# A two-block transformer layer on one core: first attention pairs loaded from the parts on chip, spills issued by ScalarE, bias load moved, sparse preparation reordered with the local keys on GpSimd

## The chip, the cores and the metric

The kernel runs on one core of a Trainium2 chip. The metric is the device time of one execution in microseconds. The kernel before takes 1689.7 us, the median of 3 runs (1689.04 to 1690.89).

## What is computed

An input x of 2 x 1024 tokens with 128 features goes through three blocks, each added to x:

```python
x = x + 0.5 * ffn(layernorm(x))     # dense attention (16 heads of 8) + mixture of experts
x = x + attn(layernorm(x))          # sparse attention: index scores, top 96 keys per query, 8 heads
x = x + 0.5 * ffn(layernorm(x))
```

`ffn` computes `h = layernorm(x + attention(x) @ w_o)`, routes each token to the best 2 of 8 experts (128 to 512 to 128, gelu) and normalizes again. `attn` scores keys with 4 small heads (relu of q.k, weighted sum), takes 64 local keys and the 32 best others, and attends over these with a compressed key and a rotated part: softplus of a projection, turned by an angle that depends on the position. All data are fp32.

## The kernel before, in words

The program runs a dense block (`c` = 0), the sparse block, and the dense block again (`c` = 1). Each engine has its own instruction list in a fixed order, written out by hand; semaphores tie them together. SP's queue issues nearly all DMAs, in the order of `sp_ffn` and `sp_sel`, and a wait of SP holds back every DMA behind it.

**Dense block.** The tokens are normalized and turned, then projected. `act_ffn` copies each projection's high part to `qparts`/`kparts` (L1244) and VectorE computes the low part (L1621, `low_done`); the values are copied by ScalarE (L1250, `va_ready`). Attention runs over 16 pairs of heads (8 per batch, `PAIRS`) with a ring of 4 buffers `QB`, `KB`, `VS`. In the buffers each head has 32 rows, the products of two parts of q with two parts of k, and 3 rows for the maxima. The rows are got by way of memory: `sp_spill` (L492) writes all parts of one batch to `q_rows` and `k_rows` (L496, L497), and `sp_rows` (L466) reads a pair back, repeated (L475, L476), with three zero rows (L477) and the values (L482). SP spills batch 0, waits for it, loads pairs 0 and 1, spills batch 1, and loads pairs 2 and 3. GpSimd (`pool_fill`) clears the buffers first (`filled`).

Per pair TensorE computes the scores once for the maxima (`pe_pass1`, L772, L779; 9 units), VectorE reduces them (`dve_max`, L1468, L1478; L1486 gives the row maxima), GpSimd splits the maxima into three bf16 parts, TensorE turns them, ScalarE copies them (`act_maxrow`, L1218), and `sp_maxrows` (L485) loads them with two small DMAs (L489) into the ring buffer. Then TensorE computes the shifted scores (`pe_scores`, L805), ScalarE the exponentials (L1209), GpSimd cuts the diagonals (L711), and TensorE multiplies with the values (`pe_values`, L827). Before the loop, pass 1 runs for 9 units of pair 0 and 4 of pair 1. In the loop, pass 1 of pair `it + 2` runs beside the scores of pair `it`.

After attention come the projection, a normalization, the gate and the experts. ScalarE waits for the experts' biases (`bb1_loaded`), which `sp_sel_loads` loads in the first block (L566, L567, five DMAs of single elements), before it turns the second normalization. The first two experts' weights are loaded at the kernel's start, for `c` = 1 as soon as the sparse block is done.

**Sparse block, preparation.** Queries are made in four rounds (`pe_raw_queries`, `act_round`, `act_log`, `dve_magnitudes` L1808, `pe_swap` L1105, `dve_rotated` L1817 to L1823, `sp_round` L600): the softplus is split into |x|, a log of exp (`act_log`, two table loads and two passes) and a maximum; `sp_round` places the four heads' parts into `QALL` with 16 DMAs of 128 KB. `pe_index`, `act_index` (L1400) and `dve_select` (L1840, L1871 to L1875) score and select keys; their units with negative places run in the preparation. The keys by row (`KVS`) go to memory for the gathers. The keys by column (`KTB`, `KTR`, a part of `QALL`) are turned by `dve_local_keys` (L1788) on VectorE after the selection of the second tile and before rounds 2 and 3; it waits for `kt_log`. GpSimd waits for the stored keys and the first indices, and then issues the gathers (L750). The main loop (`pe_keys`, `pe_scored`, ...) starts when all queries are placed.

The lines that set this order in the preparation of VectorE:

```python
for u in early[1][1:]:
    dve_select(dve, u)
dve_local_keys(dve)
for n in range(B, 2 * B):
    dve_magnitudes(dve, n)
    dve_rotated(dve, n)
```

## Time and profile before

| | |
|---|---|
| median of 3 runs | 1689.7 us |
| the profiled execution's own time | 1688.96 us |
| its span, first to last instruction | 1686.8 us |
| TensorE (matmul) / VectorE / ScalarE / GpSimd busy | 83% / 74% / 58% / 27% of the span |
| first dense block, attention | 0 to 303 us |
| sparse block | 535 to 1156 us, main loop from 685 |
| second dense block, attention | 1157 to 1450 us |
| chain that ended last | PE 55%, DVE 13%, ACT 10%, DMA 6%, issue 6%, SPq 5% |

PE is TensorE's matmul and PEld its weight load, DVE VectorE, ACT ScalarE, POOL GpSimd, SP the engine that issues DMAs; an engine's name with q is its instruction queue, whose DMA issues are not busy time. The chain is the profile's own: from the last instruction back to what released each step. A releaser is inferred. L12 is line 12 of the kernel. Times in the trace are microseconds from the span's start.

### The profile page before, as it was taken

The numbers are of one execution on the slowest core, as the hardware profiler recorded it, in microseconds if no ns is written. First come the engines' busy times: TensorE is split into PE (matmuls) and PEld (weight loads), VectorE is DVE, ScalarE is ACT, GpSimd is POOL, SyncE is SP. The second block draws the span as 40 slices with busy tenths as digits, with TensorE's granted clock in tenths as the row PEclk, the third lists the DMA queues.
The fourth block names the chain that finished last, engine by engine and source line by source line (L and its number), as shares of the span: only waits on it lengthen the run. The fifth ranks groups of instructions, "written<-read, shape, count | busy, mean of one in ns | idle before, by whom it ended". The sixth has DMA issues, their size and how long they took to land.

```text
span 1686.8 us, 31737 instructions
## 1 busy us (share of the span) xinstructions
PE 1401.3 (83%) x10664; PEld 915.3 (54%) x10664; DVE 1243.8 (74%) x2568; ACT 976.6 (58%) x1788; POOL 447.8 (27%) x751
## 2 busy tenths in 40 slices
PE   3599999799994754789999989996399999799994
PEld 2355554577773311456656655675255555577773
DVE  4578886698778577677878887754478887488787
ACT  2166666478883672346455555552166666488883
POOL 4122222100002023245455445622222233100000
PEclk9599999799997965899899999997599999799998
DMA  5211110022202244122122122212311110022200
GB/s 143 95 48 45 43 47 11 1 102 76 75 26 78 47 121 112 30 61 61 36 80 73 38 61 63 74 36 81 110 33 47 46 47 18 2 102 75 75 25 25
DMA packets 65020, 99.72 MB, mean 59 GB/s; under 512 B 21109, under 2 KB 44853, under 8 KB 62840
## 3 DMA queue, kind: packets, MB, share of 16 engines
q1 hardware_dynamic: 55254, 80.43, 15.5%
q0 software_dynamic: 8192, 16.79, 3.9%
q8 instruction: 75, 1.23, 0.3%
q10 hardware_dynamic: 1440, 0.80, 0.2%
q14 instruction: 59, 0.47, 0.1%
HBM read 73.39 MB, written 10.69 MB: 50 GB/s over the span
## 4 chain that ended last, share of the span: by engine, by line
PE 55%; DVE 13%; ACT 10%; DMA 6%; issue 6%; SPq 5%; DVEq 4%; ACTq 1%; POOL 0%; POOLq 0%
PE twin L973 8%; PE twin L963 5%; PE twin L827 5%; PE twin L1142 5%; PE twin L805 5%; DMA ffn<-arena 4%; PE twin L772 4%; ACT arena L1209 4%; DVEq L1830 2%; ACT experts L1279 2%; PE twin L1170 2%; PE twin L1158 2%; PE twin L1123 2%; PE twin L1186 2%; ACT arena L1277 2%
## 5 line engine op out<-in xcount | busy, mean ns | idle before, releaser
L1209 ACT ACTIVATE arena<-twin 128x1024 f32<-128x1024 f32 x288 | 293.8, 1024 | 172.7 <-PE twin L805 170.8
L750 POOL DMA_INDIRECT arena<-kv_rows,IDX x256 | 251.6, 983 | 309.9 <-PE twin L1189 151.0
L1478 DVE TENSOR_REDUCE arena<-twin 128x8 f32<-128x1024 f32 (+1 forms) x160 | 195.3, 1225 | 77.2 <-PE twin L772 42.9
L1277 ACT ACTIVATE arena<-twin,bias 128x512 f32<-128x512 f32 x256 | 184.9, 722 | 60.6 <-PE twin L963 60.6
L1527 DVE TENSOR_TENSOR experts<-arena,experts 128x512 fp32r<-128x512 f32 x256 | 170.1, 689 | 61.8 <-ACT experts L1279 60.5
L963 PE MATMUL twin<-experts,experts 128*128 128x512 f32 x768 | 197.0, 403 | 6.1 <-ACT experts L1279 6.1
L772 PE MATMUL twin<-ffn,ffn 64*128 64x128 f32 (+3 forms) x1152 | 154.8, 351 | 50.5 <-DMA arena<-arena 27.7
L1468 DVE TENSOR_REDUCE arena<-twin 128x2 f32<-128x1024 f32 x128 | 152.9, 1222 | 51.8 <-PE twin L772 48.4
L1279 ACT ACTIVATE experts<-twin,bias 128x512 fp32r<-128x512 f32 x256 | 186.2, 727 | 0.0
L973 PE MATMUL twin<-experts,experts 128*128 128x512 f32 x768 | 183.3, 390 | 1.0 <-DVE experts L1527 1.0
L711 POOL TENSOR_SCALAR_AFFINE_SELECT arena<-arena 128x256 f32<-128x256 f32 x256 | 99.6, 407 | 307.6 <-ACT arena L1209 307.6
L805 PE MATMUL twin<-ffn,ffn 64*128 64x128 f32 (+3 forms) x960 | 148.4, 373 | 27.7 <-DMA ffn<-arena 22.7
L963 PEld LDWEIGHTS twin<-experts,experts 128*128 128x128 f32 x768 | 143.2, 192 | 51.1 <-ACT experts L1279 23.7
L973 PEld LDWEIGHTS twin<-experts,experts 128*128 128x128 f32 x768 | 143.9, 188 | 32.9 <-issue 2.6
L827 PE MATMUL twin<-arena 128*32 128x128 f32 (+3 forms) x1920 | 159.2, 432 | 2.6 <-POOL arena L711 1.6
L645 POOL TENSOR_TENSOR rstd<-vareps,neghalf 128x8 f32<-128x8 f32 x14 | 23.4, 1674 | 511.7 <-DVE vareps L1457 511.7
L772 PEld LDWEIGHTS twin<-ffn,ffn 64*128 64x128 f32 x1152 | 96.7, 201 | 83.9 <-ACT arena L1209 36.1
L805 PEld LDWEIGHTS twin<-ffn,ffn 64*128 64x128 f32 x960 | 79.2, 188 | 109.0 <-issue 62.4
L1894 DVE TENSOR_TENSOR HN<-twin,RT 96x512 f32<-96x512 f32 x128 | 86.9, 680 | 59.1 <-PE twin L1142 51.4
L1429 ACT ACTIVATE ATT<-twin,col 128x256 f32<-128x256 f32 x128 | 60.6, 473 | 104.9 <-DVE col L1903 104.0
L1435 ACT ACTIVATE ATT<-ATT,inverse 128x256 f32<-128x256 f32 x128 | 64.6, 505 | 81.3 <-DVE inverse L1908 80.8
L1142 PE MATMUL twin<-XN,arena 128*128 128x512 bf16 x408 | 104.2, 395 | 0.2 <-DVE HN L1894 0.2
(258 smaller groups left out, 2186.6 us busy)
## 6 DMA issues: line engine op xcount, KB each, us to landing
arena<-wt_rows SPq DMA_DIRECT2D x16, 1024.0 KB, 4.8
arena<-in_L_ffn_w SPq DMA_DIRECT2D x32, 256.0 KB, 5.2
ffn<-q_rows SPq DMA_DIRECT2D x64, 128.0 KB
ffn<-k_rows SPq DMA_DIRECT2D x64, 128.0 KB
XT<-idx_rows SPq DMA_DIRECT2D x16, 512.0 KB, 4.1
q_rows<-ffn SPq DMA_DIRECT2D x8, 512.0 KB, 4.9
k_rows<-ffn SPq DMA_DIRECT2D x4, 1024.0 KB, 9.2
arena<-HN SPq DMA_DIRECT2D x32, 128.0 KB, 2.4
```

The source lines that it names most:

```text
L750: pool.indirect_dma_start(G[d % GR][:, g, :], None, kv_rows, bass.IndirectOffsetOnAxis(ap=IDX[:, q, k * GB + g:k * GB + g + 1], axis=0))\
L772: m = pe.matmul(bank[2 * slot + s][:, at * P:(at + blocks) * P], QB[buf][r, q * P:(q + 1) * P], KB[buf][r, k0 * P:(k0 + blocks) * P], star ...
L805: x = pe.matmul(bank[2 * slot + s][:, at * P:(at + 4 - p) * P], KB[buf][r, kc * P:(kc + 1) * P], QB[buf][r, (4 * g + p) * P:(4 * g + 4) * ...
L827: m = pe.matmul(bank[6][r:r + STRIP, p * P:], VS[buf][:, v:v + STRIP], PT[(UNITS * buf + u) % PT_RING][:, s, at * P:(at + 4 - p) * P], sta ...
L963: m = pe.matmul(bank[f][:, :], W1R[buf][w][:, f * P:(f + 1) * P], XR[x][:, tb * BANK:(tb + 1) * BANK], start=((w, x) == pairs[0]), stop=(( ...
L973: m = pe.matmul(bank[4 + k][:, :], W2R[buf][w][:, f, :], H1R[k][x][:, f, :], start=(f == 0 and (w, x) == pairs[0]), stop=(f == FC - 1 and ...
L1142: m = pe.matmul(o[:, :], TAB[part][:, 4 * b + c, :], OH[OH_AT[x][c] % OHR][:, :], start=(c == 0 and part == 0), stop=(c == n - 1 and part ...
L1209: act.activation(PT[(UNITS * buf + u) % PT_RING].rearrange("p s n -> p (s n)"), twin[2 * u % S_RING][:, :], ACT.Exp, scale=float(HD) ** -0 ...
L1277: act.activation(H1[tb % 2][:, f, :], bank[f][:, :], ACT.Gelu_apprx_tanh, bias=bias1[buf][:, f:f + 1])
L1279: act.activation(H1R[tb % 2][0][:, f, :], bank[f][:, :], ACT.Gelu_apprx_tanh, bias=bias1[buf][:, f:f + 1]).then_inc(gelu_done, 1)
L1478: dve.tensor_reduce(to, scores.rearrange("p (s t k) -> p s t k", s=2, t=to.shape[2]), AX_X, ALU.max).then_inc(max_done, 1)
L1527: dve.tensor_tensor(H1R[tb % 2][1][:, f, :], H1[tb % 2][:, f, :], H1R[tb % 2][0][:, f, :].bitcast(F32), ALU.subtract)\
```

## The change

It does six things.

1. The first four pairs of each dense block are no longer read back from memory. `sp_first` copies them from `qparts` and `kparts` on chip to `QB` and `KB`, eight DMAs of 16 rows (64 KB) per pair, each as soon as the low parts that it needs are ready. For pairs 0 and 1 the rows have semaphores of their own (`first_loaded`), and the values follow when both pairs' rows are issued; TensorE waits for the values in front of the first `pe_values`. The order on SP is: pairs 0, 1, their values, pair 2 with values, the maxrows of pair 0, pair 3 with values. The zero rows aren't loaded for these pairs.
2. The spill of both batches is issued by ScalarE (`act_spill`), behind its value copies and ahead of `act_maxrow(0)`. SP waits for it in front of the loop over the other pairs.
3. The bias load moves from the start to the end of the first block's attention in SP's order (`sp_biases`). In block 2 the loads of the first two experts' weights move behind pair 3.
4. For `c` = 1, buffer 0 is filled by ScalarE (`act_fill`) and not by GpSimd, and GpSimd drains before it waits for the sparse block's end.
5. In the sparse preparation the swap of round 0, the log of round 0, round 1 of the queries and its log, and the log of the keys change places with index and select units.
6. The local keys move from VectorE (16 instructions of 512 columns) to GpSimd (`pool_local_keys`, 8 instructions of 1024 columns), in front of the gathers; SP's rounds 2 and 3 wait for them.

```diff
+FIRST_LOADS = 16 * 2 * 2 * PARTS
+VISITS = PAIRS // RING
+
+def rows_target(c, buf, visit):
+
+    first = 16 if buf < 2 else 16 + FIRST_LOADS
+    return (ROW_LOADS * (VISITS - 1) + first) * c + first + ROW_LOADS * visit
...
+        def sp_parts(sp, it, s, which, done):
+            h, n = slice((2 * it + s) * HD, (2 * it + s + 1) * HD), HD * PARTS
+            for i in range(PARTS):
+                r = TILE * s + i * n
+                if which == 0:
+                    to, rows = QB[it], qparts[h, i, 0:L].unsqueeze(1).broadcast_to([HD, PARTS, L])
+                else:
+                    to, rows = KB[it], kparts[h, :, 0:L]
+                sp.dma_start(to[r:r + n, :].bitcast(F32), rows.bitcast(F32)).then_inc(done, 16)
+        def sp_values(sp, it, buf):
+            va = VA[:, :, :, :, :].rearrange("p a s k d -> p (a s k d)")
+            n = 2 * TB * VW
+            sp.dma_start(VS[buf][:, 0:n], va[:, bass.ds(it * n, n)]).then_inc(rows_loaded[buf], 16)
+        def sp_first(sp, c, it, done):
+            if c and it == 0:
+                sp.wait_ge(first_filled, 1)
+            else:
+                sp.wait_ge(filled, RING * c + it + 1)
+            for which in range(2):
+                sp.wait_ge(low_done, 8 * c + 2 * (which + 1))
+                for s in range(2):
+                    sp_parts(sp, it, s, which, done)
...
-        def sp_spill(sp, c, b):
...
         def sp_ffn(sp, c):
-            if c:
-
-                sp.wait_ge(x_ready, 2)
-                sp_expert(sp, c, 0, 0)
-                sp_expert(sp, c, 1, 1)
-
             if c == 0:
                 sp.wait_ge(zeroed, 1)
                 sp.dma_start(zero_rows, PT[0][0:MAXROWS, :, :].rearrange("p s n -> p (s n)")).then_inc(zero_stored, 16)
-            sp_spill(sp, c, 0)
+            for it in range(2):
+                sp_first(sp, c, it, first_loaded[it])
+            sp.wait_ge(va_ready, NG * (c + 1))
+            for it in range(2):
+                sp_values(sp, it, it)
             sp.wait_ge(zero_stored, 16)
-            sp.wait_ge(rows_spilled[0], (PARTS + 1) * 16 * (c + 1))
-            for k in range(RING):
-                if k == 2:
-                    sp_spill(sp, c, 1)
-                sp.wait_ge(filled, RING * c + k + 1)
-                sp_rows(sp, c, k, k)
-            sp.wait_ge(rows_spilled[1], (PARTS + 1) * 16 * (c + 1))
+            sp_first(sp, c, 2, rows_loaded[2])
+            sp_values(sp, 2, 2)
             sp_maxrows(sp, c, 0, 0)
+            sp_first(sp, c, 3, rows_loaded[3])
+            sp_values(sp, 3, 3)
+            if c:
+                for e in range(2):
+                    sp_expert(sp, c, e, e)
+            for b in range(B):
+                sp.wait_ge(rows_spilled[b], (PARTS + 1) * 16 * (c + 1))
             with sp.Fori(1, PAIRS // RING) as i:
                 for k in range(RING):
                     sp_maxrows(sp, c, i * RING + k - (RING - 1), (k + 1) % RING)
                     sp_rows(sp, c, i * RING + k, k)
             for it in range(PAIRS - RING + 1, PAIRS):
                 sp_maxrows(sp, c, it, it % RING)
+            if c == 0:
+                sp_biases(sp)
...
         def sp_round(sp, n):
...
             if n >= B:
 
+                sp.wait_ge(kl_ready, 1)
                 sp.wait_ge(qr_ready, 2 * (n + 1))
...
             if c:
-
+                pool.drain()
                 pool.wait_ge(x_ready, 2)
...
-                pool.memset(QB[buf][:, :].bitcast(F32), 0.0)
-                pool.memset(KB[buf][:, :].bitcast(F32), 0.0)
...
+                if c == 0 or buf:
+                    pool.memset(QB[buf][:, :].bitcast(F32), 0.0)
+                    pool.memset(KB[buf][:, :].bitcast(F32), 0.0)
...
+            pool_local_keys(pool)
...
+        def pool_local_keys(pool):
+            lo, mid = P // 2, P // 2 + DR
+            pool.wait_ge(kt_log, 1)
+            pool.wait_ge(rot_ready, 1)
+            for b in range(B):
+                pool.tensor_tensor(KTB[:, b, :], KTB[:, b, :], KTR[:, b, :], ALU.add)
+            pool.drain()
+            for b in range(B):
+                up, down, far = QALL[lo:mid, NH // 2 + 2 + b, 0:L], QALL[mid:, NH // 2 + 2 + b, 0:L], QALL[lo:mid, NH // 2 + b, 0:L]
+                pool.tensor_tensor(up, up, ROT[lo:mid, 0, :], ALU.mult)
+                pool.tensor_tensor(far, down, ROT[mid:, 1, :], ALU.mult)
+            pool.drain()
+            for b in range(B):
+                up, far = QALL[lo:mid, NH // 2 + 2 + b, 0:L], QALL[lo:mid, NH // 2 + b, 0:L]
+                m = pool.tensor_tensor(KL[ROWKV:, b, LW:], up, far, ALU.add)
+            m.then_inc(kl_ready, 1)
+            pool.drain()
...
-                pe.wait_ge(rows_loaded[buf], ROW_LOADS * (PAIRS // RING * c + visit + 1))
+                if isinstance(it, int) and it < 2:
+                    pe.wait_ge(first_loaded[it], FIRST_LOADS * (c + 1))
+                else:
+                    pe.wait_ge(rows_loaded[buf], rows_target(c, buf, visit))
...
                 pe_next(pe, c, 1, 1, u, u + EARLY, 0)
+            for it in range(2):
+                pe.wait_ge(rows_loaded[it], rows_target(c, it, 0))
...
+            pe_swap(pe, 0)
             for u in early[0:NIH]:
                 pe_index(pe, u)
-            pe_swap(pe, 0)
             for q in range(4):
                 if q < 2:
                     pe.wait_ge(qt_ready, q + 1)
...
                     m = pe.matmul(bank[2 + q % 2][:, t * P:t * P + ROWKV], XT[:, (4 * q + t) * P:(4 * q + t + 1) * P], WKV[:, :],
                                   start=True, stop=True)
                 m.then_inc(kv_done, 1)
+            pe.wait_ge(kv_c, 4)
+            pe_raw_queries(pe, 1)
             for u in early[NIH:]:
                 pe_index(pe, u)
-            pe.wait_ge(kv_c, 4)
-            pe_raw_queries(pe, 1)
...
+        def act_fill(act):
+            act.wait_ge(x_ready, 2)
+            for rows in (QB[0], KB[0]):
+                act.activation(rows[:, :], spare[:, 0:1].broadcast_to([P, L]), ACT.Copy)
+            act.drain()
+            for s in range(2):
+                r = slice(TILE * s + PRODS, TILE * s + ROWS)
+                m = act.activation(KB[0][r, :], neghalf[r, 0:1].broadcast_to([ROWS - PRODS, L]), ACT.Copy, scale=-2.0)
+            m.then_inc(first_filled, 1)
+        def act_spill(act, c):
+            for b in range(B):
+                act.wait_ge(low_done, 8 * c + 8 // B * (b + 1))
+                pairs, t = slice(b * (PAIRS // B), (b + 1) * (PAIRS // B)), slice(b * L, (b + 1) * L)
+                for r in range(PARTS):
+                    act.dma_start(q_rows[pairs, :, r].rearrange("j s d t -> (j s) d t"), qparts[:, r, t].bitcast(F32)).then_inc(rows_spilled[b], 16)
+                act.dma_start(k_rows[pairs].rearrange("j s d r t -> (j s d) r t"), kparts[:, :, t].bitcast(F32)).then_inc(rows_spilled[b], 16)
         def act_ffn(act, c):
             n_turn = (0, 4)[c]
+            if c:
+                act_fill(act)
...
                 m.then_inc(va_ready, 1)
+            act_spill(act, c)
             act_maxrow(act, c, 0)
...
-                if n == 3:
+                if n == 1:
                     act_log(act, (MU[0],)).then_inc(mu_log, 1)
             act.wait_ge(sg_ready, 1)
             act.wait_ge(padded, 1)
...
                 act.activation(KVS[:, rows, 0:2 * DR], src[:, :, 0:2 * DR], ACT.Abs)
                 act.activation(KVS[:, rows, 2 * DR:ROWKV], src[:, :, 2 * DR:ROWKV], ACT.Copy)
                 act.activation(KVR[:, rows, :], src[:, :, 0:2 * DR], ACT.Relu).then_inc(kv_c, 1)
+            act_round(act, 1)
+            for u in early[NIH:2 * NIH]:
+                act_index(act, u)
             act_log(act, (KVS[:, :, 0:2 * DR],)).then_inc(kv_log, 1)
-            for u in early[NIH:]:
+            act_log(act, (MU[1],)).then_inc(mu_log, 1)
+            for u in early[2 * NIH:]:
                 act_index(act, u)
-            act_round(act, 1)
-            act_log(act, (MU[1],)).then_inc(mu_log, 1)
...
+            for u in early[0][2:8]:
+                dve_select(dve, u)
             dve.wait_ge(kv_log, 1)
             dve.tensor_tensor(KVS[:, :, 0:2 * DR], KVS[:, :, 0:2 * DR], KVR, ALU.add).then_inc(kv_ready, 1)
-            for u in early[0][2:]:
+            for u in early[0][8:]:
                 dve_select(dve, u)
             dve_magnitudes(dve, 1)
             dve_select(dve, early[1][0])
             dve_rotated(dve, 1)
             for u in early[1][1:]:
                 dve_select(dve, u)
-            dve_local_keys(dve)
```

## Rows read from the trace of the kernel before

**Rows 1.** Waits, engine PE: engine line waited for, total us, times, longest us.
```profile
PE twin L772 <- DMA arena<-arena: 27.7, 2, 14.2
...
PE twin L805 <- DMA ffn<-arena: 22.7, 7, 10.8
```

**Rows 2.** Timeline, 0 to 110 us: start us, us, engine, line, operation, [idle before it].
```profile
22.54 2.62 SPq L566 DMA_DIRECT2D biases<-in_L_ffn_bb  x4
...
24.76 0.69 DVE L1621 TENSOR_TENSOR ffn<-twin,ffn 128x512 fp32r<-128x512 f32 x1 [0.17 <-ACT ffn L1244]
...
28.46 3.48 ACT L1250 ACTIVATE arena<-twin 128x128 f32<-128x128 f32 x16 [0.29 <-PE twin L889]
...
45.33 1.65 PE L772 MATMUL twin<-ffn,ffn 64*128 64x512 f32 x6 [14.23 <-DMA arena<-arena]
```

**Rows 3.** Chain that ended last: start us, us, what; DMA pieces run to their landing.
```profile
27.71 7.07 DMA k_rows<-ffn
38.64 6.56 DMA arena<-arena
...
60.68 9.11 DMA ffn<-arena
...
99.08 2.21 DMA ffn<-arena
...
673.74 4.99 DMA arena<-XN
```

**Rows 4.** Timeline, 58 to 102 us.
```profile
59.42 0.27 ACT L1218 ACTIVATE arena<-twin 48x128 f32<-48x128 bf16 x1 [27.48 <-PE twin L788]
...
69.84 0.80 PE L805 MATMUL twin<-ffn,ffn 64*128 64x512 f32 x2 [10.46 <-DMA ffn<-arena]
```

**Rows 5.** Windows: length; PE, PEld, DVE, ACT, POOL busy; clock, DMA share, GB/s.
```profile
32.00:34.00 2.00, 0.00 (x0) 0.00 (x0) 0.00 (x0) 0.00 (x0) 1.84 (x4) 1.00 0.87 354
...
62.00:64.00 2.00, 0.00 (x0) 0.00 (x0) 0.00 (x0) 0.00 (x0) 0.00 (x0) 0.50 0.15 56
...
72.00:74.00 2.00, 1.74 (x12) 1.12 (x12) 1.74 (x3) 1.33 (x2) 0.42 (x1) 0.50 0.00 0
```

**Rows 6.** Timeline of the second block's start, 1144 to 1225 us.
```profile
1175.76 3.48 ACT L1250 ACTIVATE arena<-twin 128x128 f32<-128x128 f32 x16 [0.29 <-PE twin L889]
...
1191.83 1.65 PE L772 MATMUL twin<-ffn,ffn 64*128 64x512 f32 x6 [13.43 <-DMA arena<-arena]
...
1205.86 0.27 ACT L1218 ACTIVATE arena<-twin 48x128 f32<-48x128 bf16 x1 [26.62 <-PE twin L788]
...
1216.59 0.80 PE L805 MATMUL twin<-ffn,ffn 64*128 64x512 f32 x2 [10.76 <-DMA ffn<-arena]
```

**Rows 7.** Timeline of the sparse preparation, 600 to 705 us.
```profile
615.72 1.91 ACT L1292 ACTIVATE arena<-arena 64x2048 f32<-64x2048 f32 x1
...
624.30 1.06 ACT L1292 ACTIVATE ATT<-ATT 128x1024 f32<-128x1024 f32 x1
...
625.68 0.69 DVE L1794 TENSOR_TENSOR arena<-arena 64x512 f32<-64x512 f32 x1
...
637.62 1.29 DVE L1808 SCALAR_TENSOR_TENSOR ATT<-twin,ATT 128x512 f32<-128x512 f32 x2
...
652.86 1.29 DVE L1808 SCALAR_TENSOR_TENSOR ATT<-twin,ATT 128x512 f32<-128x512 f32 x2
...
671.84 2.50 SPq L600 DMA_DIRECT2D arena<-XN  x4
...
684.98 1.94 PE L1136 MATMUL twin<-const,arena 128*128 128x128 f32 x8 [18.80 <-DVE arena L1728]
```

**Rows 8.** Page, part 6, DMA issues: count, KB each, us to landing.
```profile
arena<-HN SPq DMA_DIRECT2D x32, 128.0 KB, 2.4
```

**Rows 9.** Timeline, 520 to 612 us, engine POOL.
```profile
547.62 1.52 POOL L735 CAST maskb<-arena 128x1280 bf16<-128x1280 f32 x1
```

**Rows 10.** Page, part 5, costliest groups: count, busy us, mean ns, idle before.
```profile
L711 POOL TENSOR_SCALAR_AFFINE_SELECT arena<-arena 128x256 f32<-128x256 f32 x256 | 99.6, 407 | 307.6 <-ACT arena L1209 307.6
```

49 lines of the change are left out of this document (14 added, 35 removed).

## The prediction, made before the change was run

> **What bounds the kernel now.** I first read the list of waits, engine PE: two of its largest sums are transfers, 27.7 us in two waits of L772 and 22.7 us in seven of L805 [rows 1]. The long ones occur once per dense block, at its start, so I read the timeline there, then the chain of waits to see whether they lie on it.
>
> First block. ScalarE copies the last projection (V) until 28.46+3.48 = 31.94 (the last va_ready), and TensorE starts pass 1 only at 45.33 [rows 2]. Between them lie: SP busy with the bias DMAs from 22.54, the spill, its landing (7.07 us from the k_rows issue at 27.71) at 34.8, the row loads of pairs 0 and 1, and the landing of the values issued at 38.64 [rows 2, 3]. All these are in the chain. Then nine and four units of pass 1 (pairs 0 and 1) are paced by VectorE's maxima. ScalarE copies the turned maxima at 59.42, but L805 runs only at 69.84: the two small maxrow DMAs take 9.11 us from the second issue, while later pairs take 2.21 [rows 3, 4]. While they wait, the mean busy share of the 16 DMA engines is 0.15, against 0.87 while the spill lands [rows 5]. 0.15 of 16 is 2.4 engines: a backlog on very few engines, not a full bus. The second block repeats it: V copied by 1175.76+3.48 = 1179.24, pass 1 at 1191.83, maxima out at 1205.86+0.27 = 1206.13, L805 at 1216.59 [rows 6].
>
> Sparse preparation. The chain runs through VectorE from 625.68 (dve_local_keys) to 637.62, where dve_magnitudes(2) starts, though ScalarE had its input ready at 624.30+1.06 = 625.36. From there rounds 2 and 3 follow: 652.86 magnitudes(3), then SP's placing DMAs one after another, landed 4.99 us after the issue at 673.74, and the main loop at 684.98 [rows 3, 7].
>
> **Direct loads of the first pairs.** Removed from the path: spill, its landing, and the reload. Added: eight SBUF-to-SBUF DMAs of 64 KB per pair on SP. Nearest row: placing copies of 128 KB on SP cost 2.50/4 = 0.6 us of issue each and land in 2.4 us [rows 7, 8]. First block: the biases leave SP's queue at 22.54, the zero row store takes 0.5, so SP is ready at 23.0. Q parts wait for the second low half, two units before the fourth, about 23.7, then 4 x 0.6 = 2.4 to 26.2; the K parts' low halves are done at 24.76+0.69 = 25.45 [rows 2], so K follows to 28.6 and lands at 28.6+2.4 = 31.0. That is before 31.94, so the V copy becomes what comes last: pass 1 at 32.2 instead of 45.33, that is 13.1 saved. Second block: the same counting puts the last K copy at about 1178.5, before 1179.24; pass 1 at 1179.5 instead of 1191.83, 12.3 saved. The bounds: if the copies land as slowly as the values did (6.56 [rows 3]) the start is 35.2 and 3 us per block are lost; the V copy excludes more gain than counted.
>
> Pair 1 is wanted nine maxima later (45.33 to about 55 before, so near 42 now). Its eight issues end at 33.6 and land near 36 to 38. The values of pairs 0 and 1 now follow at 35; they are needed only at the first pe_values, so moving them costs nothing. Pair 2 is issued by 40, pair 3 after the maxrow DMAs, by 53, needed near 75. The expert weights of block two, moved behind these, are needed 200 us later. Nothing waits for them.
>
> Here the question is how many engines one such copy uses, since that decides the backlog. The rows show the k_rows reload as the thing queued on about two engines [rows 5]. The Trainium skill, DMA: Bandwidth & Descriptors, section Why a DMA increments its semaphore by 16 and not by 1, says that a copy runs on the largest number up to 16 that divides both patterns' slowest dimension. By that rule the k_rows reload (slowest dimension 2) runs on two engines, with which the trace agrees, and the new copies (8 source rows) on eight; the sum would stay as it stands.
>
> **The maxrow wait.** The copy of the maxima is now at 59.42+0.27-13.1 = 46.6. In front of the maxrow DMAs on SP there is nothing pending (pair 2 landed near 43; no k_rows reload). The spill (4 MB) is now on ScalarE's queue from 31.94. At the 354 GB/s that the spill reached [rows 5], 4 MB and the 1.1 MB of pairs 1 and 2 with values take 5.1/0.354 = 14.4 us: gone at about 47 to 48. A normal maxrow load takes two issues and 2.21, together about 3.1 from the copy [rows 3]. So L805 at about 50 instead of 69.84: 7.0 more. Second block: 1206.13+3.1 = 1209.3 against 1216.59, 7.3 more. Bounds: it still waits as long as before (0 gained), or all 7 come back. I take all, since the few-engine backlog is absent. Per block 13.1+7.0 = 20.1 and 12.3+7.3 = 19.6, together 39.7.
>
> **Spill issued by ScalarE.** Behind it on ScalarE is act_maxrow(0), wanted at 46.3. Six issues of 0.6 to 1.5 us are about 5.6 us, 31.94 to 37.5; a full queue can stretch this to perhaps 43. Then it costs nothing; if the cover is gone, a few us. The first reader of the spilled rows is pair 4, after pair 0's values.
>
> **Fill of buffer 0 on ScalarE, early drain on GpSimd.** Four copies of 1024 columns, about 1 us each, while VectorE normalizes the input (7 us) and ScalarE would only wait; hidden. GpSimd fills buffer 1 before SP, busy with pair 0 until about 1176, gets to it. Cost 0 to 1.
>
> **Bias load** at the end of the first block's attention: five issues (3.2 us) on an SP that next waits for the expert weights' table; ScalarE needs it some 15 us later. Cost 0.
>
> **Sparse preparation.** Removed from VectorE: 637.62-625.68 = 11.9 us on the path [rows 7]. Reordered: the swap of round 0 before the index units, the log of round 0 two copies earlier, round 1 before the second index group. I followed these: rotated(0) gains 3.5, but the KVS log delays the second index group, ScalarE must still do two logs before the last four index units, and the K turn starts only about 1 us sooner. So local keys' input (kt_log, before 615.72+1.91 = 617.6) comes at 616.7, and magnitudes(2) starts at about 624.6 instead of 637.62: 13.0. The bounds of the reordering alone are 0 and 3.5; I take 1.1.
>
> Added on GpSimd: eight two-input instructions of 1024 columns, for which the trace has no row. Bounds from the nearest: the cast, 1.52 for 1280 columns, gives 1.2 each, 10 us [rows 9]; the affine selection, 407 ns for 256 columns, gives 1.6 each, 13 us [rows 10]; twice the latter, since there are two inputs, 26 us. I take 13, the fp32 row: kl_ready near 630 (627 to 643). It gates SP's round 2, which needs rotated(2) anyway, done just before magnitudes(3), now at 652.86-13 = 639.9. So it is hidden except at the upper end, where 3 are lost. The gather behind it on GpSimd starts there; the main loop wants its first two loads at 672, 40 us later. The Trainium skill, GPSIMD Engine Reference, section Performance versus the Vector engine, gives 4.5 us for such an instruction of 2048 columns: estimated 18 us in all, kl_ready at 635, still hidden.
>
> Net 12: 13 less 1 for instructions of VectorE and GpSimd that may hold each other up.
>
> **Sum.** 39.7 + 12 = 51.7 on the profiled execution's 1688.96 (span 1686.8 and 2.2 around it): 1637.3. The median of the runs is 0.7 above it: 1638.
>
> **Rivals.**
> 1. The sparse gain is mostly lost: GpSimd's adds and multiplies and VectorE's two-input ones slow each other, so that kl_ready or magnitudes(3) comes late. Four two-input operations of VectorE in round 2, each held up by 1.2 us, and kl_ready at 643 (3 us) give 8 lost: 1646. Against: the rest of round 2 reads PSUM. Chance 0.17. The Trainium skill, SBUF — State Buffer, section SBUF: two separate sides, states such an exclusive lock between the two engines; no row here shows it.
> 2. The maxrow load still waits, now behind the spill, or ScalarE stands in its own full queue: 5 to 7 lost per block, 1648 to 1652. For: 4 MB are in flight at 46. Against: the bus carries 354 GB/s. Chance 0.13.
> 3. More than counted: the granted clock stays at its upper level after the short waits. The stretch after 69.84 ran at 0.50 [rows 5], its matmuls up to twice as long; I estimate 2 us per block, and with a reordering worth 3.5 that gives 1631. Chance 0.12.
> 4. Slower: a direct copy is served by one engine. One engine of the late backlog carried 56/2.4 = 23 GB/s [rows 5], so 64 KB take 2.8 us, a pair 22. Pair 0 lands at 48, pair 1 at 70 (wanted at 57), and the maxrow load stands behind pair 2 until 92 instead of 69.84: 22 later per block, less 12: 1690+44-12 = 1722. With three pairs in front of the maxrow load it turns slower above 1.8 us a copy. Against: [rows 8], the same kind of copy at 2.4 us. Chance 0.03.
> 5. The change does not do what it says, for instance pass 1 waits for something I missed at 45; 12 remains, or nothing: 1678 to 1690. Chance 0.02.
>
> The forecast, 1632 to 1644, has 0.53. The range reaches from 1628 to 1652. It takes in most of rivals 1 to 3 and leaves out 4 and 5. A measurement of this kernel can tell about 0.2% (3.4 us) from no change; faster 0.96, same 0.01, slower 0.03.
>
> **What would show it.** Pass 1 at about 32 and, in the second block, 12 us sooner after the V copy; the wait of L805 for its transfer at 3 to 4 us each; the k_rows issues on ScalarE's queue; eight GpSimd TENSOR_TENSOR of 1.2 to 3.3 us; magnitudes(2) right behind the selection's last step; the main loop near 652 on the new clock of time (684.98-20-13). Wrong would be: a wait of L772 for its rows above 3 us, a wait of SP's round 2 on GpSimd, or ScalarE's maxrow copy late.

## The result, and the profile after

The changed kernel takes 1669.99 us (median of 4 runs, 1667.76 to 1671.85), the kernel before 1690.05 us beside it (4 runs): a ratio of 0.9881, 95% interval 0.9864 to 0.9898. The gain is 20 us where 52 were forecast, and the time lies outside the range of 1628 to 1652.

The page of after, its first parts:

```profile
span 1666.0 us, 31709 instructions
...
PE 1392.9 (84%) x10630; PEld 911.5 (55%) x10664; DVE 1235.5 (74%) x2552; ACT 980.9 (59%) x1792; POOL 463.5 (28%) x755
...
PE 54%; DVE 12%; ACT 10%; issue 6%; SPq 6%; DMA 4%; DVEq 4%; POOL 1%; ACTq 1%; POOLq 0%
```

The waits of TensorE in after, from 20 to 75 us (us in total, times, longest), which answer to [rows 1]:

```profile
PE twin L827 <- DMA ffn<-ffn: 11.9, 2, 8.6
PE twin L860 <- DMA ffn<-arena: 5.2, 1, 5.2
```

L827 is pass 1 (L772 before), L860 the scores (L805 before). The longest wait of pass 1 fell from 14.2 to 3.31 us, but a second one of 8.6 us is new. The timeline of TensorE and ScalarE in after, first block (start, us, instruction, idle before), which answers to [rows 2, 3]:

```profile
34.32 1.06 PE L827 MATMUL twin<-ffn,ffn 64*128 64x512 f32 x6 [3.31 <-DMA ffn<-ffn]
...
52.96 1.65 PE L827 MATMUL twin<-ffn,ffn 64*128 64x512 f32 x6 [8.60 <-DMA ffn<-ffn]
...
55.80 0.29 PE L843 MATMUL twin<-ident_b,arena 128*128 128x128 bf16 x1
56.12 0.27 ACT L1275 ACTIVATE arena<-twin 48x128 f32<-48x128 bf16 x1 [24.28 <-PE twin L843]
61.29 0.80 PE L860 MATMUL twin<-ffn,ffn 64*128 64x512 f32 x2 [5.21 <-DMA ffn<-arena]
```

Pass 1 starts at 34.32 instead of 45.33, and then stands at pair 1 until 52.96. The transpose of pair 0's maxima (L843) comes behind pair 1's four units in TensorE's order, so it is held back too: the maxima are copied at 56.12, not at 46.6 as forecast, and the first scores start at 61.29, not at 50. Why pair 1 is late stands in the two DMA queues of after, SP's and ScalarE's:

```profile
23.72 22.21 SPq L484 DMA_DIRECT2D ffn<-ffn  x16
45.97 4.68 SPq L489 DMA_DIRECT2D arena<-arena  x2
50.77 6.73 SPq L484 DMA_DIRECT2D ffn<-ffn  x8
...
58.17 1.64 SPq L520 DMA_DIRECT2D ffn<-arena  x2
...
31.05 0.66 ACTq L1311 DMA_DIRECT2D q_rows<-ffn  x1
...
32.40 3.38 ACTq L1312 DMA_DIRECT2D k_rows<-ffn  x1
35.82 3.58 ACTq L1311 DMA_DIRECT2D q_rows<-ffn  x2
39.42 2.89 ACTq L1312 DMA_DIRECT2D k_rows<-ffn  x1
```

The 16 direct copies of pairs 0 and 1 (L484) take 22.21 us of SP's time. The eight of pair 0 are issued in 6.7 (0.67 to 1.14 each). The eight of pair 1, from 30.55 on, take 15.4, while the spill is issued and in flight: two still take 0.67 and 0.71, one 1.09, and five 1.84 to 3.04. SP then still has values and pair 2 in front of the maxrow load (L520), which it issues at 58.17, 1.8 us behind the copy of the maxima (56.39).

The second block repeats it: pass 1 at 1167.82, a wait of 8.91 us for pair 1 until 1186.76, first scores at 1195.58. Before, the first scores came 37.3 us behind the last V copy [rows 6], now 30.2 us behind it (1165.35): 7.1 gained of 19.6 forecast.

The account against before, from the starts of the same instructions in both traces (the last line is the span itself):

| | before | after | change, total | forecast, total |
|---|---|---|---|---|
| pass 1, block 1 | 45.3 | 34.3 | -11.0 | -13.1 |
| first scores, block 1 | 69.8 | 61.3 | -8.6 | -20.1 |
| last scores, block 1 | 298.3 | 293.3 | -5.0 | -20.1 |
| first compressed-query matmul | 548.5 | 541.3 | -7.2 | -20.1 |
| main loop of the sparse part | 685.0 | 670.3 | -14.7 | -32 |
| first scores, block 2 | 1216.6 | 1195.6 | -21.0 | -51.7 |
| span | 1686.8 | 1666.0 | -20.8 | -51.7 |

So the dense blocks gave about 7 us each (20.1 and 19.6 forecast), the sparse preparation 7 (12 forecast). Single landmarks carry a noise of 1 to 3 us. In four more traces with the same instructions up to there (three of them of kernels with an edited sparse part) pair 1 is late as well and the first scores of block 1 start at 61.6 to 64.5. The stretch from first to last scores takes 228.3 to 232.3 us in them; it takes 228.4 before and 232.0 here, so the 3.6 us that seem to be lost on the way are within that noise.

### The profile page after: what moved, and what is told of

It reads as the page before. It is cut to its first block, busy times and chain, and to the rows that moved or that the text cites. A ratio compares the mean times of both kernels' runs of the same rounds, so it can differ in the third digit from the quotient of the medians.

```text
span 1666.0 us, 31709 instructions
## 1 busy us (share of the span) xinstructions
PE 1392.9 (84%) x10630; PEld 911.5 (55%) x10664; DVE 1235.5 (74%) x2552; ACT 980.9 (59%) x1792; POOL 463.5 (28%) x755
## 3 DMA queue, kind: packets, MB, share of 16 engines
q8 instruction: 75, 1.23, 0.3%
## 4 chain that ended last, share of the span: by engine, by line
PE 54%; DVE 12%; ACT 10%; issue 6%; SPq 6%; DMA 4%; DVEq 4%; POOL 1%; ACTq 1%; POOLq 0%
PE twin L1030 9%; PE twin L1020 5%; PE twin L882 5%; PE twin L1199 5%; PE twin L860 5%; PE twin L827 4%; DMA ffn<-arena 4%; ACT arena L1266 3%; SPq L484 3%; DVEq L1897 3%; ACT experts L1359 2%; PE twin L1227 2%; PE twin L1215 2%; PE twin L1180 2%; ACT arena L1357 2%
## 5 line engine op out<-in xcount | busy, mean ns | idle before, releaser
L1266 ACT ACTIVATE arena<-twin 128x1024 f32<-128x1024 f32 x288 | 294.1, 1024 | 165.9 <-PE twin L860 164.1
L1560 DVE TENSOR_REDUCE arena<-twin 128x8 f32<-128x1024 f32 (+1 forms) x160 | 195.4, 1225 | 67.6 <-PE twin L827 33.2
L827 PE MATMUL twin<-ffn,ffn 64*128 64x128 f32 (+3 forms) x1152 | 154.7, 351 | 44.5 <-DMA ffn<-ffn 24.1
L860 PE MATMUL twin<-ffn,ffn 64*128 64x128 f32 (+3 forms) x960 | 149.4, 376 | 17.8 <-DMA ffn<-arena 13.6
L827 PEld LDWEIGHTS twin<-ffn,ffn 64*128 64x128 f32 x1152 | 96.3, 201 | 79.1 <-ACT arena L1266 36.2
L860 PEld LDWEIGHTS twin<-ffn,ffn 64*128 64x128 f32 x960 | 79.9, 190 | 100.9 <-issue 63.9
L1199 PE MATMUL twin<-XN,arena 128*128 128x512 bf16 x374 | 96.1, 395 | 5.9 <-issue 5.2
## 6 DMA issues: line engine op xcount, KB each, us to landing
ffn<-q_rows SPq DMA_DIRECT2D x48, 128.0 KB
ffn<-k_rows SPq DMA_DIRECT2D x48, 128.0 KB
```

What stands on the lines that cost most here:

```text
L827: m = pe.matmul(bank[2 * slot + s][:, at * P:(at + blocks) * P], QB[buf][r, q * P:(q + 1) * P], KB[buf][r, k0 * P:(k0 + blocks) * P], star ...
L860: x = pe.matmul(bank[2 * slot + s][:, at * P:(at + 4 - p) * P], KB[buf][r, kc * P:(kc + 1) * P], QB[buf][r, (4 * g + p) * P:(4 * g + 4) * ...
L1199: m = pe.matmul(o[:, :], TAB[part][:, 4 * b + c, :], OH[OH_AT[x][c] % OHR][:, :], start=(c == 0 and part == 0), stop=(c == n - 1 and part ...
L1266: act.activation(PT[(UNITS * buf + u) % PT_RING].rearrange("p s n -> p (s n)"), twin[2 * u % S_RING][:, :], ACT.Exp, scale=float(HD) ** -0 ...
L1560: dve.tensor_reduce(to, scores.rearrange("p (s t k) -> p s t k", s=2, t=to.shape[2]), AX_X, ALU.max).then_inc(max_done, 1)
```

## Experiments: the dense blocks

**Theory A**: the spill, started at 31 in the middle of pair 1's copies, holds these back. **Rival B**: the direct copies are slow by themselves; while they run alone (25 to 31 us) the 16 DMA engines are busy to 0.44 of their time. The second question is whether an earlier start stays gained. The experiments ran on several chips. Some grant TensorE a lower clock in the sparse main loop (a mean granted clock of 0.88 of 2.4 GHz from 700 to 900 us in the changed kernel again, 0.96 in its first trace), so that the kernel before takes 1810 to 1816 us there; ratios are to the kernel before on the same chip, and landmarks up to the end of block 1 can be compared directly.

### The spill behind pair 3

```diff
-            act_spill(act, c)
...
             sp_values(sp, 3, 3)
...
             for b in range(B):
+                sp_spill(sp, c, b)
+            for b in range(B):
                 sp.wait_ge(rows_spilled[b], (PARTS + 1) * 16 * (c + 1))
```

> The spill leaves ScalarE's queue and is issued by SyncE behind pair 3's values, so that nothing else is in flight while pairs 0 and 1 are copied. Theory A (the spill holds the copies back): the eight copies that took 0.67 to 1.14 us each before the spill are the rule, pair 1's eight are issued from 31 to about 39 and land by 43; TensorE's wait of 8.6 us for pair 1 falls under 1.5 us, the first scores start at 54 to 56 instead of 61.29, the same in the second block: 6 us each, about 1657 to 1660 us. Rival B (the copies are slow by themselves, since only about half of the 16 DMA engines serve them): pair 1's copies stretch to 2 or 3 us each without the spill too, the wait stays at 7 us or more, and the time stays within 3 us of 1670.

Ratio 0.9914 (0.988 to 0.9948): the time missed theory A's (some 0.981) and is not told apart from the changed kernel's 0.9881. The timeline of that run, SP and TensorE (L836 is pass 1, L869 the scores):

```profile
23.18 13.10 SPq L484 DMA_DIRECT2D ffn<-ffn  x16
...
47.14 1.64 SPq L520 DMA_DIRECT2D ffn<-arena  x2
...
62.54 2.50 SPq L528 DMA_DIRECT2D k_rows<-ffn  x1
72.39 1.70 SPq L520 DMA_DIRECT2D ffn<-arena  x2
...
32.97 1.48 PE L836 MATMUL twin<-ffn,ffn 64*128 64x512 f32 x6 [2.97 <-DMA ffn<-ffn]
...
50.28 0.80 PE L869 MATMUL twin<-ffn,ffn 64*128 64x512 f32 x2 [3.48 <-DMA ffn<-arena]
...
75.71 0.79 PE L869 MATMUL twin<-ffn,ffn 64*128 64x512 f32 x2 [8.37 <-DMA ffn<-arena]
```

Theory A holds for the copies and B falls: the same 16 copies take 13.10 us instead of 22.21, the wait for pair 1 is gone, the maxima are copied at 46.84 (forecast 46.6) and the first scores start at 50.28 (forecast 50). It is the bytes in flight that stretch the issues, and not ScalarE issuing at the same time: in the changed kernel ScalarE's last issue ends at 42.31, and SP's next three, from 43.13 on, still take 2.80, 2.54 and 2.10 us; the spill's last landing is at 53.33. Every edit of the spill's place here and below also moves it to SP's queue, so what a late spill from ScalarE's queue would do was not tested. But almost nothing is left of the earlier start: block 1's last scores are at 290.1, against 291.3 of the changed kernel's dense blocks on the same chip (the dense-only run below). The edit made a wait of its own: the load of pair 1's maxima (L520 at 72.39) stands on SP behind the wait for the spill's landing, and TensorE stands 8.37 us.

### The maxima's rows ahead of pair 2

```diff
+            sp_maxrows(sp, c, 0, 0)
             sp_first(sp, c, 2, rows_loaded[2])
             sp_values(sp, 2, 2)
-            sp_maxrows(sp, c, 0, 0)
```

> Only SyncE's order is changed: the maxima's rows of pair 0 are loaded ahead of the copies of pair 2. In the changed kernel the maxima were copied at 56.1 and their load was issued at 58.2, behind pair 2's last copies. Theory A: the first scores start 2 us earlier in each block, about 1666 us, and pair 1 is still waited for 8.6 us. Rival (pair 2 becomes the late one, since SyncE now stands for the maxima): pair 2's rows land 8 to 10 us later and TensorE waits for them in the loop, 1670 to 1675 us.

Ratio 0.9911 (0.9873 to 0.9949), not told apart from 0.9881. The load is issued 0.1 us behind the copy of the maxima (58.33) instead of 1.8, and the wait of the scores falls from 5.21 to 3.64 us. Pair 1 came 1.9 us later than in the changed kernel in this trace (54.82), so the first scores are at 61.59. The order on SP is worth 1.6 us in that wait, not the loss.

> Both edits: the spill behind pair 3, the maxima's rows ahead of pair 2. Theory A: pair 1 lands by 43, the maxima are copied at 48 to 50 and loaded at once, the first scores start at 51 to 53 instead of 61.29: 9 us a block, about 1651 to 1654 us. Rival B (copies slow by themselves): about 1665 us, the 2 us of the order alone.

Ratio 1.0014 (0.999 to 1.0039), a miss: the first scores are at 50.42, no earlier than with the late spill alone, since SP was already free in time there (L520 at 47.13 against 47.14). Pairs 2, 3 and the spill moved back instead, SP reached the load of pair 1's maxima only at 79.80, and TensorE stood 15.35 us at 83.13. Block 1's last scores: 297.8, where the kernel before has 298.3.

### The load of pair 1's maxima ahead of the wait

```diff
                 sp_spill(sp, c, b)
+            sp_maxrows(sp, c, 1, 1)
...
-                    sp_maxrows(sp, c, i * RING + k - (RING - 1), (k + 1) % RING)
                     sp_rows(sp, c, i * RING + k, k)
+                    sp_maxrows(sp, c, i * RING + k - (RING - 2), (k + 2) % RING)
```

> As the run with the late spill, but the load of pair 1's maxima's rows is taken out of the loop and issued between the spill's last issue and the wait for its landing (the loop's order is otherwise kept). In the run with the late spill SyncE stood in that wait until 72.4 us and TensorE waited 8.4 us for the rows. Theory A: that wait goes, the first scores stay at 50.3, the last scores of the first block end at 281 to 283 instead of 290.1 (293.3 in the changed kernel), the second block gains the same 10 to 11 us against the changed kernel; in all 1648 to 1652 us on a chip that gives the changed kernel 1670. Rival (what is saved at the start is given back within the loop by a lower granted clock or by late rows of pairs 2 to 4): the last scores stay at 288 or later.

Ratio 0.9868 (0.9825 to 0.991), the changed kernel itself on that chip 0.9878 (0.9838 to 0.9919): no clear difference, where theory A had 0.987 to 0.989 of the changed kernel's time. The load is now issued at 67.19, behind the spill's issues, and still waited for (5.5 us; 7.2 in block 2). Last scores of block 1 at 286.2, 6.6 us ahead of the changed kernel on that chip. In block 2 the first scores came 17.2 us behind pass 1's start instead of 28.1, and the attention behind them took 241.1 us instead of 228.6: all given back.

### The spill in two parts

Pair 1's maxima go ahead of the spill; batch 0 is spilled behind them, batch 1 behind pair 4's rows.

```diff
+            sp_maxrows(sp, c, 1, 1)
+            sp_spill(sp, c, 0)
+            sp_maxrows(sp, c, 2, 2)
+            sp.wait_ge(rows_spilled[0], (PARTS + 1) * 16 * (c + 1))
+            sp_rows(sp, c, 4, 0)
+            sp_spill(sp, c, 1)
+            for k in range(1, RING):
+                sp_rows(sp, c, RING + k, k)
+                sp_maxrows(sp, c, RING + k - 2, (k + 2) % RING)
```

> The mended late spill still cost a wait of 5.5 us for pair 1's maxima's rows in the first block and 7.2 us in the second, since their load was issued at 67.2 behind the spill (TensorE wanted it at about 65), and the granted clock stayed at 0.70 to 0.73 there until 1345 in the second block. Here that load goes ahead of the spill, batch 0 is spilled behind it, batch 1 only behind the rows of pair 4, and the second block's expert loads behind those of pair 7. Theory A: the first scores at 50 to 52, no wait for the maxima's rows of pair 1 above 1.5 us, last scores of the first block at 281 to 283 (292.8 in the changed kernel on this chip, 286.2 in the mended run), from the first to the last scores of the second block 229 to 232 us instead of 241: 10 us a block against the changed kernel, ratio to the kernel before 0.976 to 0.980. Rival (the loop gives the early start back whatever the spill does): last scores at 286 or later, ratio 0.985 or more.

Ratio 0.9879 (0.9853 to 0.9904), the rival's number. The wait has only moved on to pair 3's maxima: their load was issued at 96.58 behind pair 5's rows and batch 1's spill, and it landed late. SP's timeline in that run (L528 spills k, L511 reads k's rows back, L520 loads the maxima), and TensorE's with the wait (L875 is the scores):

```profile
87.89 1.53 SPq L528 DMA_DIRECT2D k_rows<-ffn  x1
...
94.70 0.66 SPq L511 DMA_DIRECT2D ffn<-k_rows  x1
...
96.58 1.62 SPq L520 DMA_DIRECT2D ffn<-arena  x2
...
103.72 0.79 PE L875 MATMUL twin<-ffn,ffn 64*128 64x512 f32 x2 [5.48 <-DMA ffn<-arena]
```

And the windows around it (length; busy us and instructions of PE, PEld, DVE, ACT, POOL; granted clock, DMA share, GB/s):

```profile
94.00:98.00 4.00, 3.68 (x47) 2.05 (x45) 3.18 (x3) 2.94 (x4) 0.77 (x2) 1.00 0.42 149
98.00:104.00 6.00, 0.52 (x10) 0.28 (x4) 0.50 (x1) 0.14 (x1) 0.77 (x2) 0.93 0.11 43
104.00:108.00 4.00, 3.76 (x24) 1.81 (x23) 1.86 (x2) 2.12 (x3) 0.00 (x0) 0.50 0.10 29
108.00:112.00 4.00, 4.00 (x26) 3.16 (x26) 1.81 (x2) 2.36 (x3) 0.82 (x2) 0.50 0.30 89
112.00:116.00 4.00, 4.00 (x26) 1.66 (x22) 2.65 (x3) 1.02 (x1) 0.77 (x2) 0.50 0.11 42
116.00:120.00 4.00, 3.68 (x35) 2.07 (x31) 2.89 (x7) 2.22 (x4) 1.15 (x6) 0.90 0.01 2
```

This is where saved time goes. TensorE stands 5.5 us, the granted clock falls from 1.00 (2.4 GHz) to 0.50 (1.2 GHz), and for 12 us after the wait it does 24 to 26 matmuls in 4 us instead of some 45. Block 1's first to last scores take 240.0 us here, against 228.4 in the kernel before, 232.0 in the changed one and 230.9 in the next run, where this wait is gone: a wait of 5.5 us costs the block 8 to 11.5, by the nearest comparison 9.

The windows also show what the late load stood behind, and it was not the spill's bytes, whose last landing is at 96.69. From 98 to 104 the 16 DMA engines are busy to 0.11 at 43 GB/s, that is some two engines, as in the wait of the kernel before (0.15 and 56 GB/s, [rows 5]). What is left in flight are the reloads of pair 5's rows, issued until 95.90. So the few-engine backlog that the prediction held to be absent comes back as soon as a load of maxima follows the reloads closely; the spill did its harm by holding these up. Whether a reload spread over more engines would remove the wait was not tested.

### Batch 1 behind pair 3's maxima

```diff
-            sp_rows(sp, c, 4, 0)
-            sp_spill(sp, c, 1)
-            for k in range(1, RING):
+            for k in range(RING):
                 sp_rows(sp, c, RING + k, k)
-                sp_maxrows(sp, c, RING + k - 2, (k + 2) % RING)
+                if k:
+                    sp_maxrows(sp, c, RING + k - 2, (k + 2) % RING)
+                if k == 1:
+                    sp_spill(sp, c, 1)
```

> The run with the split spill had the first scores at 50.9 and no wait for pair 1's maxima, but batch 1's spill, issued at 86.6 ahead of pair 5's rows and pair 3's maxima, made that load land late: TensorE waited 5.5 us at 103.7 for it (5.6 in the second block) and ran at a granted clock of 0.73 in that stretch of 25 us where it had 1.00 otherwise. Here batch 1 is spilled behind the load of pair 3's maxima. Theory A (each 5 us of such a wait costs the block about 11 us, the wait and as much again at the lower clock): no wait above 1.5 us between the first and the last scores, block 1's last scores at 279 to 282 (290.9 in that run, 293.3 in the changed kernel), 228 to 230 us from the first to the last scores in each block; ratio to the kernel before 0.974 to 0.978. Rival (the early start is given back whatever waits are left): last scores at 288 or later, ratio 0.985 or more.

1646.02 us, ratio 0.9728 (0.9708 to 0.9749), a little better than theory A's 0.974: 24 us less than the changed kernel (0.9881), measured on another chip. First scores at 50.7, last scores of block 1 at 281.7; 230.9 and 230.8 us between them in the two blocks (228 to 230 expected). Here pair 5's rows are issued by 90.49, and the load of pair 3's maxima at 95.49. The same windows in that run:

```profile
94.00:98.00 4.00, 3.68 (x45) 2.01 (x45) 2.88 (x4) 2.66 (x4) 0.77 (x2) 1.00 0.14 51
98.00:104.00 6.00, 5.25 (x58) 3.15 (x52) 4.48 (x4) 4.32 (x6) 1.58 (x4) 1.00 0.94 310
104.00:108.00 4.00, 3.93 (x42) 1.87 (x40) 3.06 (x6) 2.32 (x3) 1.24 (x4) 1.00 0.55 148
```

The batch's 2 MB are in flight from 98 on (share 0.94), and TensorE runs at full clock beside them, because nothing that it waits for is queued behind them. The rival that an early start is given back whatever is left falls. Block 1's last scores are now 16.6 us earlier than before, of the 20.1 that the prediction had for the block.

## Experiments: the sparse preparation

Three kernels take the sparse part of the change apart; the dense blocks are those of the changed kernel.

```diff
-            pool_local_keys(pool)
...
+            dve_local_keys(dve)
             for n in range(B, 2 * B):
                 dve_magnitudes(dve, n)
```

The other two put the order of pe, act and dve back as it was, with and without the keys' move.

> The changed kernel with the sparse preparation of the kernel before (order and local keys): what the dense blocks' part gives alone. By the traces the two blocks gave 8.6 and 7.1 us, so 1674 to 1676 us here, and the main loop of the sparse part starts about 8 to 9 us earlier than before, at 676. Rival (the sparse changes cost or gave nothing): 1670 us.

> The changed kernel with the sparse order of the kernel before: of the sparse part only the move of the local keys to GpSimd is left. The interval from the first compressed-query matmul to the first matmul of the main loop was 140.7 us with neither and 131.6 with both. By the prediction's terms (11.9 of 13.0 us from the keys) it is about 132. If the reordering carries the gain and the keys' move is eaten by VectorE's stalls beside GpSimd, it is 137 to 139.

> The changed kernel with the local keys back on VectorE: of the sparse part only the reordering is left. Counted from the first compressed-query matmul, the third query round's magnitudes came at 90.8 us with neither change, at 79.0 with the keys alone, at 77.6 with both. If the two add, they come at 89 to 90 here (the prediction's 1.1 us for the order), the gathers run ahead of rounds 2 and 3 as in the kernel before, round 3 is issued in 10 us, and the main loop starts at 138 to 140 (134.5 with both, 140.7 with neither).

> The changed kernel unedited, as the comparison for the others on the same chip: 0.988 of the time of the kernel before if the chip grants the clock of the first comparison, and the same stretches at its start (first scores at 61 to 62 us).

Measured, us behind the first compressed-query matmul (ends of SP's round 3 and starts of the others; chip A is of the kind of the first comparison):

| | magnitudes(2) | magnitudes(3) | last issue of round 3 | first main-loop matmul at L1199 or its like |
|---|---|---|---|---|
| before (A) | 89.1 | 104.4 | 125.9 | 138.7 |
| neither (B) | 90.8 | 106.7 | 128.4 | 140.7 |
| order alone (A) | 90.5 | 106.4 | 128.0 | 140.6 |
| keys alone (B) | 79.0 | 94.5 | 126.9 | 134.4 |
| both, first comparison (A) | 80.0 | 95.9 | 117.3 | 131.5 |
| both, again (B) | 77.6 | 93.2 | 125.5 | 134.5 |

(Ratios: neither 0.9937, 0.9912 to 0.9962; both, again 0.9878, 0.9838 to 0.9919. The other two ran once: keys alone 1786.8 us with 1810.2 beside it, order alone 1676.9 with 1686.5.) Several expectations missed: neither gave 0.9937, a smaller gain than the 0.9905 to 0.9917 expected; keys alone put the loop at 134.4, between the 132 and the 137 of the two theories; order alone at 140.6, above its 138 to 140; and the changed kernel again had its first scores at 64.5, not at 61 to 62. On B the keys' move brings magnitudes(2) 11.8 us forward (90.8 to 79.0), the 11.9 of the forecast. The order brings another 1.4 there (79.0 to 77.6; 1.1 forecast) and nothing at the end; on A, order alone came 1.4 later than before (90.5 against 89.1). More loss is behind it: on B round 3 ends only 1.5 us earlier with the keys moved. SP's timeline in the run `both, again` (rounds 2 and 3), and below it the first gather in GpSimd's:

```profile
636.11 2.49 SPq L629 DMA_DIRECT2D arena<-arena  x4
638.64 5.67 SPq L629 DMA_DIRECT2D arena<-HN  x8
644.35 2.49 SPq L629 DMA_DIRECT2D arena<-XN  x4
647.45 5.29 SPq L629 DMA_DIRECT2D arena<-arena  x4
653.58 10.47 SPq L629 DMA_DIRECT2D arena<-HN  x8
664.83 3.68 SPq L629 DMA_DIRECT2D arena<-XN  x4
```

```profile
632.09 1.22 POOL L783 DMA_INDIRECT arena<-kv_rows,IDX  x1 [1.05 <-issue]
```

Round 3 takes 21.1 us from its first issue to the end of its last (647.45 to 668.51) instead of 10.3. The issues themselves are hardly longer, 10.3 us for the 16 in sum against 9.6 before; what grows are the pauses between them, from 0.04 to about 0.75 us each. The trace names nothing that SP waits for in these pauses. In the kernel before, GpSimd did its first 16 gathers from 619.44 on, ahead of rounds 2 and 3 (from 652.80). The local keys now occupy GpSimd until about 631, and 24 gathers run beside the rounds' copies. Before, 8 gathers ran beside round 3 too, on B (neither) as on A, and its issues took 10.2 us.

The remaining runs ask whether the gathers are the cause. First, all of them wait until round 3 has landed (edit on the kernel with the spill in two parts):

```diff
             pool.wait_ge(kv_stored, 16 * B)
+            for i in range(2):
+                pool.wait_ge(q_placed[i], 16 * 16 * B)
```

> The run before this one with one wait more on GpSimd: the gathers of the sparse part start when the last query round has landed. The local keys on GpSimd had moved the first 16 gathers from 69 to 93 us behind the first compressed-query matmul (sparse order of before) to 89 to 110, into the copies of rounds 2 and 3, and in four of five traces with the move round 3's 16 issues took 17 to 19 us instead of 10. Theory G (the gathers hold the copies back): round 3's issues take 10 to 11 us, its last ends at 116 to 118 instead of 125, the rows land by 123; the main loop may then wait for the gathers, which end 15 us later than they did. Rival (the copies of round 3 are slow for another reason): the last issue still ends at 124 to 127.

Ratio 0.9911 (0.9889 to 0.9933), by the medians 4 us worse than without the edit (0.9879, 0.9853 to 0.9904). This chip was an A: round 3 was issued in 10 us with the gathers too (last end at 117.0; 117.5 here), so the stretched issues were not put to the test. But its rows landed 3.1 us earlier, counted from the first compressed-query matmul (119.6 instead of 122.7), and then TensorE waited for the first gathers: the loop at 134.6 instead of 131.5.

Second, eight gathers go ahead and the rest wait, on the kernel with batch 1 behind pair 3's maxima:

```diff
+                    if d == 2:
+                        for i in range(2):
+                            pool.wait_ge(q_placed[i], 16 * 16 * B)
```

> The run before this one, with GpSimd's gathers from the ninth on held until the last query round has landed (eight go ahead as before; holding all of them made the rows land 4 us earlier, at 119.3 us behind the first compressed-query matmul, but the main loop then waited for the first gathers). Theory G: the rows land at 119 to 121 instead of 122.5, the main loop starts at 127 to 129 instead of 131.5 (on a chip where round 3's issues stretch to 17 to 19 us, at 129 instead of 134.5): 3 us less than the run before this one. Rival: the later gathers are waited for in the loop and the 3 us are lost again, the same time within 2 us.

1644.1 us, ratio 0.972 (0.9702 to 0.9738), the fastest of all; against 0.9728 of the run without the edit it is not told apart. In the trace the loop starts at 126.8 instead of 131.4. 1.9 of that is there before round 3 starts (it ends at 114.7 against 116.6; the clock, below); the other 2.7 go with its earlier landing (3.2 us behind the end of the last issue instead of 6.4).

> The run before this one with one step of the sparse reordering undone: the first logarithm of the query magnitudes stands behind the fourth copy of the indexer queries again instead of behind the second. From the first compressed-query matmul to the first matmul of the sparse main loop the changed kernel took 131.6 us (138.6 before). Theory S (the early logarithms, 4.7 us on ScalarE, hold back the copies that the indexer's keys wait for): the interval falls to about 129 us. Rival (round 0 of the queries is what is late): it stays at 131 to 133.

Ratio 0.9853 (0.9813 to 0.9893), not told apart from 0.9868. The miss is in the theory: the indexer's key matmuls start 17.6 us behind the first compressed-query matmul with the log behind the fourth copy, and 17.7 with it behind the second. The early log does not delay these matmuls, and the interval grew from 132.7 to 134.7 instead of falling to 129. The growth says little of the log: those eight matmuls ran in part at half clock in this trace and took 5.40 us instead of 3.60 (the clock, below).

## Why the prediction was wrong, point by point

- **Pass 1 at 32.2 (13.1 saved).** Measured 34.32 and 11.0, inside the bound of 35.2. The copies are not issued in 0.6 us each, but in 0.82 (13.10 us for 16, undisturbed), and land in 3 to 4. Block 2: 3.30 us of wait instead of none.
- **"Its eight issues end at 33.6 and land near 36 to 38."** This is the step that failed. They ended at 45.9, and pair 1 was there at 52.96 when TensorE wanted it at 44.4. The text priced the spill only for what stands behind it on ScalarE and for the maxrow load, and not for the copies on the other queue that share the DMA engines from 31 on. With the spill elsewhere the step comes nearly true (issues end at 36.3, no wait).
- **L805 at 50 (7.0 more).** It was 61.29, because of the step above: the maxima's transpose stands behind pair 1 on TensorE, and SP was busy. The maxrow load itself behaved: 3.2 us from the end of the copy in the run with the late spill, for 3.1 forecast.
- **Spill on ScalarE costs nothing.** True for ScalarE (issues until 42.3, forecast 37.5 to 43); false for SP. Rival 2 had this cause, but hung it on the maxrow load and priced it at 5 to 7 us a block. It was 12.9 and 12.5 (20.1 less 7.2, 19.6 less 7.1), since the wait sits at pair 1 and ahead of the maxrow load. The chance of 0.13 and the edge of 1652 were too small for a 4 MB transfer that no row showed beside small copies.
- **Rival 4** (one engine, 1722): the copies keep 0.44 of the engines busy while alone, so not one. That sides with the Trainium skill, DMA: Bandwidth & Descriptors, section Why a DMA increments its semaphore by 16 and not by 1, whose rule gives eight of 16 for eight source rows.
- **Fill on ScalarE, early drain, bias load.** Nothing waits for them in the trace. As forecast.
- **Sparse, 12.** Its sum was 13.0 at magnitudes(2), less 1 for engines that hold each other up; measured, on A, 9.1 there (89.1 to 80.0) and 7.2 at the main loop. Of the 3.9 that lack at magnitudes(2), some 2.4 go with four matmuls of the indexer queries at half clock (below), and 1.75 with a cast of VectorE beside GpSimd (next point). That the terms came out at 11.8 and 1.4 on B, for 11.9 and 1.1, is in part luck: in the trace of neither, VectorE waited 1.5 us longer for TensorE in the preparation than in the kernel before, and against the latter the keys' move brings 10.1. GpSimd's eight instructions took 2.34 us each (one 3.22), not 1.6, and end at 631.9, ahead of round 2 at 637.22: hidden, as said. Another 1.9 are lost behind magnitudes(2), 1.0 of them because the last copy of round 3 landed 6.00 us after its issue instead of 4.99 [rows 7]. The text followed the gathers only to their reader in the loop, "40 us later", and not to the copies that they now run beside; with the gathers held back the landing is 3.1 us earlier. What the other 0.9 are, and what stretches round 3 on B, stays open.
- **Rival 1** (VectorE and GpSimd hold each other up) is seen, and small. VectorE's timeline in after, beside GpSimd's L797 and L798:

```profile
619.44 2.03 DVE L1930 CAST bidh<-bidx 128x32 f16<-128x32 uint32 x1
622.75 2.15 DVE L1884 SCALAR_TENSOR_TENSOR HN<-ATT,arena 128x1024 f32<-128x1024 f32 x1
```

The cast took 0.28 us in the kernel before, L1884 takes 1.23 elsewhere: 2.7 us in all, the 1.75 of the cast on the path. One GpSimd instruction grew from 2.34 to 3.22 in the same stretch. The starts and ends fit turns: the cast, begun at 619.44, ends at 621.47, just behind GpSimd's instruction (621.43); L1884 starts at 622.75 while GpSimd's next runs until 623.82, and ends at 624.90, and the instruction of GpSimd that started at 623.88 in between is the one of 3.22. The Trainium skill, SBUF — State Buffer, section SBUF: two separate sides, has an exclusive lock between the two engines when VectorE reads two operands of SBUF, as L1884 does; there the trace agrees. The cast reads one, so whether the same lock held it up is not shown.

## What to carry to other kernels

A transfer that is moved to an idle engine's queue is still in the way of every transfer that starts beside it: cost it against each small copy that is due while its bytes are in flight, on whatever queue. Put bulk transfers directly behind the last small load that someone waits for, and as late as their first reader allows; here the place of 4 MB and of two small loads was worth some 24 us. A small load is late too when it follows row reloads that only about two engines carry, however idle the rest are. Where saved time does not arrive at the end, look for the next wait of the same kind, and at the granted clock right behind it. When an engine takes over work, follow what it did before (the gathers) to the transfers that it now collides with.
